# Four stages of a one-core transformer kernel: zeros sent in the first attention, scatters behind a product, slot inputs turned a span sooner, low parts a slot later

## The chip, the core and the metric

The kernel runs on one core of a Trainium2 chip. The core's engines each run their own instruction stream: TensorE (PE) multiplies matrices, VectorE (DVE), ScalarE (ACT) and GpSimd (POOL) do elementwise work, and SyncE (SP) issues most DMA transfers. They wait for each other by semaphores. The metric is the device time of one execution in microseconds. The kernel before takes 4922.42 us (median of 3 runs, 4919.28 to 4930.78).

## The reference

Four transformer layers over an activation of 4 x 1024 tokens of width 128. Each layer is `x = x + attention(norm(x)) + ffn(norm(x))`, in float32. The parts that the change touches:

- Layer 0's attention: 16 heads of width 64, softmax over 1024 keys, for 4 sequences.
- Layer 2's attention is linear: `q, k = elu(.) + 1`, `kv = k^T v`, `out = q kv / (q . sum(k) + eps)`, 16 heads of width 64.
- Layer 2's ffn is a mixture of 8 experts with top 2 and a capacity. Each token is copied to a slot of each of its two experts (at most 1024 slots per expert), the experts run over their slots, and the token gathers two weighted results:

```
disp = zeros(E * cap, D).at[flat_idx].add(x * valid)
h    = relu(disp @ fc1 + b1);  eo = h @ fc2 + b2
out  = sum(eo[flat_idx] * gates * valid)
```

- Layer 3: an attention with a recurrence over time (`S = exp(w) * S + k v`), and a mixture of 64 experts with top 8 and one shared expert, `silu(x Wg) * (x Wu)` weighted by a gate and then multiplied by `Wd`.

## The kernel before, in words

The activation is kept transposed in SBUF (`res_t`, 128 x 4096), and a normalised copy in `xn_t`. The program is a row of stages (`layer_norm`, `wide_attention`, ..., `slot_experts`, `mixing_and_experts`), each a block in which every engine has its written order of instructions, with a barrier at its end. Names in the profile have a letter for the stage: `n_` normalisation, `a_` attention, `e_` experts, `m_` the last stage. Most products are made of float16 parts: a value is split into `high` and `low`, and three matmuls (high by high, low by high, high by low) stand for one.

**Zeros.** The experts' input slots (`slots_d`, in DRAM) and their results (`y_d`) must hold zeros wherever no token lands. Between layer 0 and the second `layer_norm` a block of its own lets ACT's queue copy 4 MB of prepared rows (`slots2`) into each (L2738, L2739). `layer_norm` then loads `avg` and `ident` on SP's queue (L101, L102), and its first matmul (L114) waits for them.

**First attention** (`wide_attention`, L171). 32 units (4 sequences by 8 pairs of heads). Per unit SP issues twelve copies within SBUF (L293 to L298) that stack the parts of q and k for PE; in between SP waits.

**Linear attention** (`linear_attention`, L1057). 32 units again; `order` lists the jobs of a unit for all engines, with PE one or two units ahead in some. For unit n PE makes k, q and v (`ring`), ACT takes exponent and relu of k and q (`grown`, `clipped`), and DVE joins them (`k_s`, `q_s`, L1275), sums k over the tokens (`k_part`, L1247), and copies a product of state and output weights (`folded`, L1286). POOL multiplies q with the sum of k (`prod`, L1309); DVE reduces `prod` to the denominator and inverts it (`den`, L1254 to L1256, right behind `folded`); POOL multiplies q by it (`scaled`, two halves, L1316). PE's `state` product of the next unit waits for `folded` (L1167). Ahead of each `prod`, POOL also issues two indirect DMAs (L1302) that scatter 128 rows each of the layer's normalised tokens to their slots; they wait once for the zeros (L1299).

**Slot experts** (`slot_experts`, L2463). 8 experts, two spans of 512 slots each, and four steps per span. PE turns a span's slots (four transposes into `turned`, L2566), DVE splits it into `x_high` and `x_low` (L2666, L2668), and in each step PE makes a block of `hidden`, ACT stores it twice (`whole`, `high`), DVE makes `low` (L2679), and four steps later PE adds to `out`. The result is turned back (L2574), weighted by DVE (`y_s`, L2691) and scattered by POOL in four indirect DMAs (L2657). POOL also makes the low part of the next expert's weights (`w_low`, L2645), in the same queue. `span_at(step, j, lag)` gives the span that is due in step j of a span, `lag` spans back.

**Last stage** (`mixing_and_experts`, L1515 on). 264 steps (33 pairs of experts by 8 chunks of 512 tokens), one per slot, with the jobs of the recurrence at fixed slots between them (tables `PE_AT`, `ACT_AT`, `DVE_AT`, `POOL_AT`). Step s: PE makes gate and up products (slot s), ACT the silu (slot s, L1904), DVE the product with up (`acted`, slot s + 1, L2065), POOL the product with the gate (`scaled`, slot s + 1, L1947), ACT the high part (slot s + 2, L1898), DVE the low part (`lows`, slot s + 2, L2071), PE `out` (slot s + 4). Every third step DVE adds `out` to the activation (L1968), for which PE's next `out` waits. PE's gate product of step s waits for `acted` of step s - 2.

Of the kernel before, what the change touches and what calls it, by code (L numbers as in the profile page):

```python
# [14 lines left out]
P = 128  # L15
B, N = 4, 1024
T = B * N
# [153 lines left out]
def wide_attention(nc, stage, res_t, xn_t, w_d, w_out_d, ident_d, consts_d, scale, eps):  # L171
# [41 lines left out]
    with ExitStack() as ctx:  # L213
# [62 lines left out]
        with nc.Block() as block:  # L276
            @block.sync
            def _(eng):
# [7 lines left out]
                for n in range(units):  # L286
# [4 lines left out]
                    for h in range(2):  # L291
# [6 lines left out]
                        eng.dma_start(kb[0:64, r, h, :], nat_low["k"][own, r, :]).then_inc(stack_in[r], 16)  # L298

# [757 lines left out]
def linear_attention(nc, stage, res_t, xn_t, w_d, w_out_d, mask_d, ident_d, eps, rows, slot_of, slots_d, cleared, scattered):  # L1057
# [15 lines left out]
    with ExitStack() as ctx:  # L1073
# [51 lines left out]
        with nc.Block() as block:  # L1125
# [169 lines left out]
            def _(eng):  # L1295
# [219 lines left out]
def mixing_and_experts(nc, stage, res_t, xn_t, d, gates_d, w_d):  # L1515
# [8 lines left out]
    UP_LAG, HIGH_LAG, LAG, SPLIT_AT = 1, 2, 4, 8  # L1524
# [40 lines left out]
    with ExitStack() as ctx:  # L1565
# [105 lines left out]
        with nc.Block() as block:  # L1671
# [149 lines left out]
            def _(eng):  # L1821
# [53 lines left out]
                for slot in range(SLOTS):  # L1875
# [17 lines left out]
                    s = step_at(slot, HIGH_LAG)  # L1893
                    if s >= 0:
                        eng.wait_ge(scaled_done, s + 1)
                        if s >= HR:
                            eng.wait_ge(out_used, s - HR + 1)
                        eng.activation(high[:, s % HR, :], scaled[:, s % SR, :], ACT.Copy).then_inc(high_done, 1)  # L1898
                    s = step_at(slot, 0)
                    if s >= 0:  # L1900
# [4 lines left out]
                        if s % PER_UNIT == SPLIT_AT and s // PER_UNIT + 1 < UNITS:  # L1905
                            split(s // PER_UNIT + 1)

# [47 lines left out]
            def _(eng):  # L1955
# [101 lines left out]
                for slot in range(SLOTS):  # L2057
# [8 lines left out]
                    s = step_at(slot, HIGH_LAG)  # L2066
# [396 lines left out]
def slot_experts(nc, stage, res_t, slots_d, y_d, w_d, bias_d, ident_d, filled_sem, filled_count):  # L2463
# [7 lines left out]
    HB, HR, RING = 3, 8, 3  # L2471
# [3 lines left out]
    with ExitStack() as ctx:  # L2475
# [8 lines left out]
        x_high = pl.sb("x_high", [P, 2, BANK], F16)  # L2484
        x_low = pl.sb("x_low", [P, 2, BANK], F16)
# [27 lines left out]
        sent = [pl.sem(f"sent{r}") for r in range(2)]  # L2513
# [8 lines left out]
        with nc.Block() as block:  # L2522
# [30 lines left out]
            def _(eng):  # L2553
# [24 lines left out]
                turn_in(0)  # L2578
                for step in range(LAST):
# [16 lines left out]
                    if span_at(step, 1, -1) >= 0 and step > 0:  # L2596
                        turn_in(span_at(step, 1, -1))
# [265 lines left out]
```

## Time and profile before

| | |
|---|---|
| median of 3 runs | 4922.42 us |
| the profiled execution | 4929.4 us |
| its span | 4927.6 us |
| PE busy | 4247.0 us (86%) |
| DVE busy | 3604.9 us (73%) |
| ACT busy | 3188.9 us (65%) |
| POOL busy | 2235.6 us (45%) |

The span runs from the first to the last recorded instruction. Busy time is what an engine's instructions cover, waits left out. As the stages follow each other with barriers, the shares of the whole span say little on one stage. In the trace the second normalisation starts near 2011 us, the linear attention runs from about 3410 to 3830, the slot experts to about 4013, and the last stage from about 4050 to the end. In a row of the timeline the columns are the start and duration in us, the engine, the line and the operation, output and inputs with their shapes, how many instructions were merged, and in brackets how long the engine had been idle before, and what ended that. A queue (SPq, ACTq) issues DMAs.

### The profile page before, as it was taken

The page shows a single profiled execution, that of the slowest core. Times are in us where ns is not written, and L with a number is a line of the kernel's source. Part 1 is how long each engine was busy: PE and PEld are TensorE (multiplying, and loading weights), DVE is VectorE, ACT ScalarE, POOL GpSimd, SP SyncE. Part 2 cuts the span into 40 slices and gives each one's busy share as a digit, 9 for nine tenths or more (in the row PEclk, how much of TensorE's full clock was granted, in tenths as well). Part 3 has the DMA queues.
Part 4 walks back from the last instruction along what each step waited for, and adds up shares of the span by engine and source line. Part 5 has one row for each costly group of instructions (what it writes and reads, how often), then busy time and mean ns, then how long its engine had stood idle before and what let it go on. Part 6 is the DMA issues. An engine that isn't in the chain of part 4 may idle for free. (4 is left out here: it accounts for less than half of the span.)

```text
span 4927.6 us, 91117 instructions
## 1 busy us (share of the span) xinstructions
PE 4247.0 (86%) x35369; PEld 2321.4 (47%) x35370; DVE 3604.9 (73%) x4865; ACT 3188.9 (65%) x4796; POOL 2235.6 (45%) x1299
## 2 busy tenths in 40 slices
PE   5999999999989799677888769995877778999998
PEld 3666666666666444221211124444666343333333
DVE  5888888888845577379888947774776537888887
ACT  2777777777764599347677749992555525555554
POOL 2888888888850133200000003331555435655664
PEclk7999999999999899779999979996999879999999
DMA  2111111111100111300000011110000223334333
GB/s 62 40 40 40 40 40 41 40 39 38 37 12 1 45 65 64 104 25 14 27 18 22 14 45 44 64 43 22 12 12 13 81 81 96 90 92 100 90 96 77
DMA packets 111741, 237.30 MB, mean 48 GB/s; under 512 B 20990, under 2 KB 50942, under 8 KB 108678
## 3 DMA queue, kind: packets, MB, share of 16 engines
q1 hardware_dynamic: 98934, 214.84, 16.1%
q10 hardware_dynamic: 8304, 8.45, 0.6%
q0 software_dynamic: 4096, 8.46, 0.5%
q8 instruction: 270, 4.42, 0.4%
q14 instruction: 137, 1.11, 0.1%
HBM read 161.06 MB, written 28.75 MB: 39 GB/s over the span
## 5 line engine op out<-in xcount | busy, mean ns | idle before, releaser
L528 POOL TENSOR_TENSOR a_prob_low<-a_prob_whole,a_prob_high 128x1024 f16<-128x1024 f32 x512 | 1084.8, 2132 | 276.7 <-ACT a_prob_high L418 272.3
L502 DVE TENSOR_REDUCE a_part_max<-a_top 128x2 f32<-128x1024 f32 x512 | 626.1, 1223 | 218.5 <-PE a_top L329 212.6
L415 ACT ACTIVATE a_prob_whole<-a_score 128x1024 f32<-128x1024 f32 x512 | 525.0, 1025 | 332.5 <-PE a_score L318 320.5
L780 ACT ACTIVATE a_prob<-a_score 128x512 f32<-128x512 f32 x1024 | 532.9, 605 | 259.9 <-PE a_score L724 259.9
L813 DVE TENSOR_REDUCE a_part_max<-a_side 128x2 f32<-128x1024 f32 x512 | 595.1, 1218 | 88.1 <-PE a_side L695 88.1
L2283 DVE TENSOR_TENSOR e_low<-e_whole,e_high 128x512 f16<-128x512 f32 x544 | 453.2, 843 | 168.8 <-ACT e_high L2241 167.4
L1947 POOL TENSOR_TENSOR m_scaled<-m_acted,m_gate 128x512 f32<-128x512 f32 x264 | 402.5, 1531 | 322.3 <-DVE m_acted L2065 245.9
L418 ACT ACTIVATE a_prob_high<-a_score 128x1024 f16<-128x1024 f32 x512 | 522.3, 1020 | 0.0
L317 PE MATMUL a_score<-a_qa,a_ka 128*128 128x256 f16 x2048 | 476.2, 273 | 0.0
L318 PE MATMUL a_score<-a_qb,a_kb 128*128 128x256 f16 x2048 | 476.0, 273 | 0.0
L384 PE MATMUL a_o_ps<-a_v,a_prob_high 128*128 128x65 f16 x4096 | 428.1, 193 | 6.2 <-POOL a_prob_low L528 3.4
L2266 POOL TENSOR_TENSOR all_res_t<-all_res_t,e_gated 128x512 f32<-128x512 f32 x136 | 219.6, 1615 | 460.9 <-DVE e_gated L2292 460.6
L386 PE MATMUL a_o_ps<-a_v,a_prob_high 128*128 128x64 f16 x4096 | 426.9, 194 | 0.0
L388 PE MATMUL a_o_ps<-a_v,a_prob_low 128*128 128x65 f16 x4096 | 424.5, 192 | 0.0
L384 PEld LDWEIGHTS a_o_ps<-a_v,a_prob_high 128*128 128x128 f16 x4096 | 376.0, 96 | 85.7 <-DVE a_tokens L488 35.4
L2238 ACT ACTIVATE e_whole<-e_hidden,e_bias 128x512 f32<-128x512 f32 x544 | 383.6, 705 | 16.7 <-PE e_hidden L2190 3.0
L386 PEld LDWEIGHTS a_o_ps<-a_v,a_prob_high 128*128 128x128 f16 x4096 | 377.7, 97 | 26.9 <-issue 10.9
L2241 ACT ACTIVATE e_high<-e_hidden,e_bias 128x512 f16<-128x512 f32 x544 | 381.8, 702 | 0.0
L388 PEld LDWEIGHTS a_o_ps<-a_v,a_prob_low 128*128 128x128 f16 x4096 | 377.9, 98 | 0.0
L1898 ACT ACTIVATE m_high<-m_scaled 128x512 f16<-128x512 f32 x264 | 165.9, 628 | 288.2 <-POOL m_scaled L1947 286.1
L2071 DVE TENSOR_TENSOR m_lows<-m_scaled,m_high 128x512 f16<-128x512 f32 x264 | 239.0, 905 | 111.0 <-ACT m_high L1898 111.0
L724 PE MATMUL a_score<-a_qa,a_ka 32*128 32x512 f16 x1024 | 237.5, 398 | 90.0 <-ACT a_prob L780 87.6
(402 smaller groups left out, 10337.5 us busy)
## 6 DMA issues: line engine op xcount, KB each, us to landing
m_gate<-gates SPq DMA_DIRECT2D x264, 256.0 KB, 5.1
e_gate<-gates SPq DMA_DIRECT2D x17, 2048.0 KB, 7.1
a_ka<-a_nat_high_k SPq DMA_DIRECT2D x128, 128.0 KB, 2.4
e_w<-in_w_moe SPq DMA_DIRECT2D x25, 512.0 KB, 7.8
a_qa<-a_nat_high_q SPq DMA_DIRECT2D x64, 128.0 KB, 2.4
a_qa<-a_nat_low_q SPq DMA_DIRECT2D x64, 128.0 KB, 2.4
a_qb<-a_nat_high_q SPq DMA_DIRECT2D x64, 128.0 KB, 2.4
a_kb<-a_nat_low_k SPq DMA_DIRECT2D x64, 128.0 KB, 2.4
```

What stands on the lines that cost most here:

```text
L317: eng.matmul(score[:, e % 2, h, i, :], ka[:, r, h, keys], qa[:, r, h, qs], start=True, stop=False)
L318: mm = eng.matmul(score[:, e % 2, h, i, :], kb[:, r, h, keys], qb[:, r, h, qs], start=False, stop=True)
L384: eng.matmul(o_ps[:, at:at + V1], high, v[:, r, kt, h, 0:V1], start=(pair == 0 and i == 0 and h == 0 and t == 0), stop=False, skip_group_c ...
L386: eng.matmul(o_ps[:, at:at + DH], high, v[:, r, kt, h, V1 + 1:VW], start=False, stop=False, skip_group_check=True)
L388: mm = eng.matmul(o_ps[:, at:at + V1], low, v[:, r, kt, h, 0:V1], start=False, stop=last, skip_group_check=True)
L415: eng.activation(prob_whole[:, e % RING, :, :, :], score[:, e % 2, :, :, :], ACT.Exp, scale=scale)
L418: eng.activation(prob_high[:, e % RING, :, :, :], score[:, e % 2, :, :, :], ACT.Exp, scale=scale).then_inc(exp_done, 1)
L502: eng.tensor_reduce(part_max[:, i, c, :, qt % 4], top[:, :, :], AX.X, ALU.max).then_inc(max_done, 1)
L528: eng.tensor_tensor(prob_low[:, e % RING, :, :, :], prob_whole[:, e % RING, :, :, :], prob_high[:, e % RING, :, :, :], ALU.subtract).then_ ...
L780: eng.activation(prob[:, e % RING, h, :], score[:, step % SLOTS, :], ACT.Exp).then_inc(exp_done, 1)
L813: op = eng.tensor_reduce(part_max[:, qt // 4, c, 2 * pair:2 * pair + 2, 24 + qt], side, AX.X, ALU.max)
L2283: eng.tensor_tensor(low[:, s % HR, :], whole[:, s % HB, :], high[:, s % HR, :], ALU.subtract).then_inc(low_done, 1)
```

## The change

1. The two 4 MB copies of `slots2` no longer have a block of their own. They are cut into 16 parts of 1024 rows, and SP issues one behind the twelve stack copies of each of the units 2 to 17 of the first attention. POOL's wait in the linear attention counts 16 parts.
2. In the linear attention POOL issues `prod` ahead of the two scatters of a unit.
3. In the slot experts `turn_in` and `split_x` are done two spans ahead instead of one, `turn_in` in step 3 instead of step 1; `x_high` and `x_low` have three buffers instead of two, and `slots` four instead of three. The semaphores `sent` are now made by the caller.
4. In the last stage DVE makes `lows` of step s in slot s + 3 instead of s + 2, and ACT issues the silu of a slot ahead of the high part.

```diff
@@ wide_attention, SP
                         eng.dma_start(kb[0:64, r, h, :], nat_low["k"][own, r, :]).then_inc(stack_in[r], 16)
+                    if n >= 2:
+                        for to, source in clears[n - 2:n - 1]:
+                            eng.dma_start(to, source).then_inc(cleared, 16)
@@ linear_attention, POOL
-                eng.wait_ge(cleared, 32)
+                eng.wait_ge(cleared, cleared_count)
                 for n in range(units):
-                    for j in range(2):
-                        eng.indirect_dma_start(slots_d, bass.IndirectOffsetOnAxis(slot_of[:, j, n:n + 1], 0),
-                                               rows[:, j, n, :], None).then_inc(scattered, 16)
                     r = n % 2
                     eng.wait_ge(small_read, small["ksum", n] + 1)
...
                     eng.tensor_tensor(prod[:, :, :], q_s[:, r, :, :], k_sum[:, r, :].unsqueeze(1).broadcast_to([P, tiles, P]),
                                       ALU.mult).then_inc(multiplied, 1)
+                    for j in range(2):
+                        eng.indirect_dma_start(slots_d, bass.IndirectOffsetOnAxis(slot_of[:, j, n:n + 1], 0),
+                                               rows[:, j, n, :], None).then_inc(scattered, 16)
                     eng.wait_ge(norm, NORMS * n + 3)
@@ mixing_and_experts
-    UP_LAG, HIGH_LAG, LAG, SPLIT_AT = 1, 2, 4, 8
+    UP_LAG, HIGH_LAG, LOW_LAG, LAG, SPLIT_AT = 1, 2, 3, 4, 8
@@ mixing_and_experts, ACT: this piece moves from ahead of the silu to behind it
-                    s = step_at(slot, HIGH_LAG)
-                    if s >= 0:
-                        eng.wait_ge(scaled_done, s + 1)
...
-                        eng.activation(high[:, s % HR, :], scaled[:, s % SR, :], ACT.Copy).then_inc(high_done, 1)
@@ mixing_and_experts, DVE
-                    s = step_at(slot, HIGH_LAG)
+                    s = step_at(slot, LOW_LAG)
                     if s >= 0:
                         eng.wait_ge(high_done, s + 1)
@@ slot_experts
-    HB, HR, RING = 3, 8, 3
+    HB, HR, RING, XR = 3, 8, 4, 3
...
                 turn_in(0)
+                turn_in(1)
                 for step in range(LAST):
...
-                    if span_at(step, 1, -1) >= 0 and step > 0:
-                        turn_in(span_at(step, 1, -1))
+                    if span_at(step, 3, -2) >= 0:
+                        turn_in(span_at(step, 3, -2))
@@ slot_experts, DVE
                 def split_x(s):
-                    if s >= 2:
-                        eng.wait_ge(hidden_full, J * (s - 1))
+                    if s >= XR:
+                        eng.wait_ge(hidden_full, J * (s - XR + 1))
...
-                    if span_at(step, 2, -1) >= 0 and step > 0:
-                        split_x(span_at(step, 2, -1))
+                    if span_at(step, 2, -2) >= 0:
+                        split_x(span_at(step, 2, -2))
@@ program
+        clears = in_parts(slots_d, d["slots2"], EXPERTS * CAPACITY) + in_parts(y_d, d["slots2"][:, 0:P], 2 * T)
...
-        with nc.Block() as block:
-            @block.scalar
-            def _(eng):
-                eng.dma_start(slots_d[0:EXPERTS * CAPACITY, :], d["slots2"]).then_inc(cleared, 16)
-                eng.dma_start(y_d[0:2 * T, :], d["slots2"][:, 0:P]).then_inc(cleared, 16)
-
```

The order of the instructions, at three places. POOL at the start of the units of the linear attention, before:

```order
L1298 TENSOR_TENSOR a_w_low<-a_w,a_w_high 128x384 x8
L1302 DMA slots<-rows,slot_of 16384x130 x2
L1309 TENSOR_TENSOR a_prod<-a_q_s,a_k_sum 128x1024
L1316 TENSOR_TENSOR a_scaled<-a_q_s,a_den 128x512 x2
L1302 DMA slots<-rows,slot_of 16384x130 x2
L1309 TENSOR_TENSOR a_prod<-a_q_s,a_k_sum 128x1024
```

and now:

```order
L1301 TENSOR_TENSOR a_w_low<-a_w,a_w_high 128x384 x8
L1309 TENSOR_TENSOR a_prod<-a_q_s,a_k_sum 128x1024
L1312 DMA slots<-rows,slot_of 16384x130 x2
L1319 TENSOR_TENSOR a_scaled<-a_q_s,a_den 128x512 x2
L1309 TENSOR_TENSOR a_prod<-a_q_s,a_k_sum 128x1024
L1312 DMA slots<-rows,slot_of 16384x130 x2
```

The two scatters (`slots<-rows,slot_of`) stand between `prod` and `scaled` of a unit now, and no longer between `scaled` of the unit before and `prod`.

PE in a span of the slot experts; `e_turned` is the turning in of a coming span, `e_back` the turning back of a finished one. Before, from the middle of a step on:

```order
L2555 MATMUL e_out<-e_high,e_w_high 128x512
L2556 MATMUL e_out<-e_low,e_w_high 128x512
L2557 MATMUL e_out<-e_high,e_w_low 128x512
L2566 MATMUL e_turned<-e_ident,e_slots 128x128 x4
L2555 MATMUL e_hidden<-e_x_high,e_w_high 128x512
L2556 MATMUL e_hidden<-e_x_low,e_w_high 128x512
L2557 MATMUL e_hidden<-e_x_high,e_w_low 128x512
L2555 MATMUL e_out<-e_high,e_w_high 128x512
L2556 MATMUL e_out<-e_low,e_w_high 128x512
L2557 MATMUL e_out<-e_high,e_w_low 128x512
L2574 MATMUL e_back<-e_ident,e_o_s 128x128 x4
```

and now:

```order
L2557 MATMUL e_out<-e_high,e_w_high 128x512
L2558 MATMUL e_out<-e_low,e_w_high 128x512
L2559 MATMUL e_out<-e_high,e_w_low 128x512
L2576 MATMUL e_back<-e_ident,e_o_s 128x128 x4
L2557 MATMUL e_hidden<-e_x_high,e_w_high 128x512
L2558 MATMUL e_hidden<-e_x_low,e_w_high 128x512
L2559 MATMUL e_hidden<-e_x_high,e_w_low 128x512
L2557 MATMUL e_out<-e_high,e_w_high 128x512
L2558 MATMUL e_out<-e_low,e_w_high 128x512
L2559 MATMUL e_out<-e_high,e_w_low 128x512
L2568 MATMUL e_turned<-e_ident,e_slots 128x128 x4
```

The turning in stood one step ahead of the turning back and stands one step behind it, two steps later than before, for a span that is needed one span later.

ACT in the last stage, around a job of the recurrence (`m_low`); `m_acted` is the silu of a step. Before:

```order
L1837 ACT_TABLE_LOAD
L1837 ACTIVATE m_low<-m_work 128x512
L1898 ACTIVATE m_high<-m_scaled 128x512
L1904 ACT_TABLE_LOAD
L1904 ACTIVATE m_acted<-m_up_down 128x512
L1898 ACTIVATE m_high<-m_scaled 128x512
L1904 ACTIVATE m_acted<-m_up_down 128x512
```

and now:

```order
L1840 ACT_TABLE_LOAD
L1840 ACTIVATE m_low<-m_work 128x512
L1901 ACT_TABLE_LOAD
L1901 ACTIVATE m_acted<-m_up_down 128x512
L1909 ACTIVATE m_high<-m_scaled 128x512
L1901 ACTIVATE m_acted<-m_up_down 128x512
L1909 ACTIVATE m_high<-m_scaled 128x512
```

The silu of a slot comes ahead of the high part that stood in front of it (the first `m_high` now stands behind the second table load). DVE's rows read alike before and after there: what changes is that each `m_lows` belongs to the step before the one it belonged to.

## Rows read from the trace of the kernel before

**Rows 1.** Windows: busy us of PE, PEld, DVE, ACT, POOL; clock; DMA share; GB/s.

```profile
3440.00:3820.00 380.00, 298.81 (x3204) 248.92 (x3204) 268.07 (x316) 203.45 (x402) 222.75 (x156) 0.99 0.04 12
4130.00:4900.00 770.00, 714.35 (x2733) 300.38 (x2731) 638.35 (x830) 434.43 (x699) 460.62 (x306) 0.99 0.38 91
```

**Rows 2.** Timeline of PE, second and third normalisation.

```profile
2032.20 2.08 PE L114 MATMUL n_mean<-all_res_t,n_avg 128*128 128x512 f32 x2 [20.96 <-DMA n_ident<-in_ident]
...
3331.86 2.08 PE L114 MATMUL n_mean<-all_res_t,n_avg 128*128 128x512 f32 x2 [6.59 <-DMA n_bias<-in_bias]
```

**Rows 3.** DMA view, the second transfer of zeros: us to landing last.

```profile
y<-in_slots ACTq DMA_DIRECT2D x1, 4096.0 KB, 30.5
```

**Rows 4.** Timeline of POOL in the linear attention.

```profile
3599.58 2.37 POOL L1309 TENSOR_TENSOR a_prod<-a_q_s,a_k_sum 128x1024 f32<-128x1024 f32 x1
...
3606.42 2.81 POOL L1316 TENSOR_TENSOR a_scaled<-a_q_s,a_den 128x512 f32<-128x512 f32 x2 [4.47 <-DVE a_den L1256]
...
3611.69 2.37 POOL L1309 TENSOR_TENSOR a_prod<-a_q_s,a_k_sum 128x1024 f32<-128x1024 f32 x1
```

**Rows 5.** Timeline of ACT and DVE, same stretch and an early unit.

```profile
3609.11 0.28 ACT L1221 ACTIVATE a_k_sum<-a_small 128x128 f32<-128x128 f32 x1 [0.98 <-PE a_small L1170]
...
3610.90 0.69 DVE L1275 SCALAR_TENSOR_TENSOR a_q_s<-a_grown,a_clipped 128x512 f32<-128x512 f32 x1 [2.37 <-ACT a_clipped L1216]
...
3612.63 1.98 DVE L1275 SCALAR_TENSOR_TENSOR a_k_s<-a_grown,a_clipped 128x512 f32<-128x512 f32 x1 [1.04 <-ACT a_clipped L1216]
...
3616.53 0.28 DVE L1286 COPY a_folded<-a_small 128x128 f32<-128x128 f32 x1
...
3452.99 3.37 DVE L1275 SCALAR_TENSOR_TENSOR a_q_s<-a_grown,a_clipped 128x512 f32<-128x512 f32 x1 [2.70 <-ACT a_clipped L1216]
...
3453.96 0.60 ACT L1215 ACTIVATE a_grown<-a_ring 128x512 f32<-128x512 f32 x1 [0.51 <-PE a_ring L1158]
```

**Rows 6.** Waits of PE, 3453 to 3815: total, times, longest.

```profile
PE a_small L1167 <- DVE a_folded L1286: 41.5, 29, 2.1
```

**Rows 7.** Waits of PE in the slot experts, 3840 to 3990.

```profile
PE e_hidden L2555 <- issue: 13.4, 6, 2.2
PE e_hidden L2555 <- DVE e_x_low L2668: 12.5, 10, 2.3
```

**Rows 8.** Timeline of DVE, POOL and PE in the slot experts.

```profile
3900.84 0.68 DVE L2691 TENSOR_TENSOR e_y_s<-e_back,e_slots 128x512 f32<-128x512 f32 x1
...
3906.61 2.14 POOL L2645 TENSOR_TENSOR e_w_low<-e_w,e_w_high 128x1024 f16<-128x1024 f32 x1
...
3908.85 0.38 PE L2555 MATMUL e_hidden<-e_x_high,e_w_high 128*128 128x512 f16 x1 [2.23 <-issue]
...
3916.55 0.68 DVE L2691 TENSOR_TENSOR e_y_s<-e_back,e_slots 128x512 f32<-128x512 f32 x1
```

**Rows 9.** Source line of the scatters: ns min/median/max, first and last start.

```profile
L2657 POOL DMA_INDIRECT y<-e_y_s,e_dest x63: 952/959/1430, 3867.1 to 3988.9; - x63
```

**Rows 10.** Waits of DVE and PE in the last stage, 4130 to 4900.

```profile
DVE m_lows L2071 <- ACT m_high L1898: 106.3, 101, 3.7
PE m_out L1725 <- DVE all_res_t L1968: 20.0, 20, 3.2
PE m_up_down L1725 <- DVE m_acted L2065: 17.3, 37, 1.6
```

**Rows 11.** The page's part 5, POOL's line in the last stage.

```profile
L1947 POOL TENSOR_TENSOR m_scaled<-m_acted,m_gate 128x512 f32<-128x512 f32 x264 | 402.5, 1531 | 322.3 <-DVE m_acted L2065 245.9
```

**Rows 12.** Timeline of DVE and PE in the last stage.

```profile
4745.22 1.09 DVE L2071 TENSOR_TENSOR m_lows<-m_scaled,m_high 128x512 f16<-128x512 f32 x1 [1.23 <-ACT m_high L1898]
...
4748.96 0.39 PE L1725 MATMUL m_up_down<-m_x_high,m_w_high 128*128 128x512 f16 x1
...
4750.26 1.02 PE L1798 MATMUL m_work<-m_mixed,m_w_v 128*128 128x512 f32 x2
...
4752.55 0.39 PE L1725 MATMUL m_out<-m_high,m_w_high 128*128 128x512 f16 x1 [1.27 <-DVE all_res_t L1968]
```

More of the change, by code:

```diff
@@ L168, in layer_norm, with wide_attention @@
         pl.close()
-def wide_attention(nc, stage, res_t, xn_t, w_d, w_out_d, ident_d, consts_d, scale, eps):
+def wide_attention(nc, stage, res_t, xn_t, w_d, w_out_d, ident_d, consts_d, scale, eps, clears, cleared):
     GROUPS, DH = 8, 64
@@ L1054, in whole_attention, with linear_attention @@
         pl.close()
-def linear_attention(nc, stage, res_t, xn_t, w_d, w_out_d, mask_d, ident_d, eps, rows, slot_of, slots_d, cleared, scattered):
+def linear_attention(nc, stage, res_t, xn_t, w_d, w_out_d, mask_d, ident_d, eps, rows, slot_of, slots_d, cleared, cleared_count, scattered):
     PAIRS, DH = 8, 64
@@ L1906, in _ @@
                             split(s // PER_UNIT + 1)
+                    s = step_at(slot, HIGH_LAG)
+                    if s >= 0:
+                        eng.wait_ge(scaled_done, s + 1)
+                        if s >= HR:
+                            eng.wait_ge(out_used, s - HR + 1)
+                        eng.activation(high[:, s % HR, :], scaled[:, s % SR, :], ACT.Copy).then_inc(high_done, 1)
             @block.gpsimd
@@ L2483, in slot_experts @@
         dest = pl.sb("dest", [P, E, PER * TILES], U32)
-        x_high = pl.sb("x_high", [P, 2, BANK], F16)
-        x_low = pl.sb("x_low", [P, 2, BANK], F16)
+        x_high = pl.sb("x_high", [P, XR, BANK], F16)
+        x_low = pl.sb("x_low", [P, XR, BANK], F16)
         whole = pl.sb("whole", [P, HB, BANK])
@@ L2587, in _ @@
                             eng.wait_ge(high_done, step - HB + 1)
-                        product(hidden[:, step % HB, :], j, s // PER % 2, (x_high[:, s % 2, :], x_low[:, s % 2, :]), True, True).then_inc(hidden_full, 1)
+                        product(hidden[:, step % HB, :], j, s // PER % 2, (x_high[:, s % XR, :], x_low[:, s % XR, :]), True, True).then_inc(hidden_full, 1)
                     k = step - LAG
@@ L2716, in program @@
         scattered = pl.sem("scattered")
+        sent2 = [pl.sem(f"sent2{r}") for r in range(2)]
         slots_d = nc.dram_tensor("slots", (EXPERTS * CAPACITY + 2 * T, P + 2), F32, kind="Internal").ap()
@@ L2724, in _, with in_parts @@
                 eng.wait_ge(x_in, 16)
+        def in_parts(to, source, rows):
+            part = 2 * BANK
+            return [(to[at:min(at + part, rows), :], source[at:min(at + part, rows), :]) for at in range(0, rows, part)]
+        clears = in_parts(slots_d, d["slots2"], EXPERTS * CAPACITY) + in_parts(y_d, d["slots2"][:, 0:P], 2 * T)
         layer_norm(nc, "n0", res_t, xn_t, d["avg"], d["ident"], d["bias0"])
-        wide_attention(nc, "a0", res_t, xn_t, d["w_qkv0"], d["w_o0"], d["ident"], d["rowmask0"], scale=64 ** -0.5, eps=1e-10)
+        wide_attention(nc, "a0", res_t, xn_t, d["w_qkv0"], d["w_o0"], d["ident"], d["rowmask0"], scale=64 ** -0.5, eps=1e-10,
+                       clears=clears, cleared=cleared)
         with nc.sbuf_tensor("xp_t", [P, T], F32) as xp_t:
```

14 lines of the change are left out of this document (6 added, 8 removed).

## The prediction

> **What bounds the kernel now.** I read the busy time by stretch first [rows 1]. The kernel is a row of stages with a barrier between them, so each edit is priced in its own stage. DMA bounds neither of the two long stretches: its share is 0.04 and 0.38. In the linear attention (3440 to 3820) no engine is full: PE is busy for 299 of 380 us. In the last stage (4130 to 4900) PE is busy for 714.35 of 770, so 55.65 us are idle, and it is the nearest to a PE bound. Then I read, in each, who ends PE's waits and what that one was doing, which is where the terms below come from.
>
> **1. The zeros leave the gap before the second normalisation.** The first matmul of n1 comes after 20.96 us of idle PE, ended by the load of a 64 KB constant; in n2, which follows the same kind of stage, the gap is 6.59 [rows 2]. The difference is two transfers of 4 MB each, issued ahead of that load; the second lands 30.5 us after its issue [rows 3]. Without them n1's gap should be n2's: 20.96 - 6.59 = 14.4 us less. It is a plain serial gap, nothing else runs in it. Bounds: 13 (the constants are issued a little later than in n2) to 15.
>
> They now go out as 16 parts of about 0.5 MB on SP's queue in the first attention, one behind the twelve copies of a unit. Both transfers together took 30.5 us, so a part takes about 1.9 us (30.5 / 16), and the next unit's copies are a whole unit away. SP stands idle there and nobody waits for a part until the scatters. I take 0. If each part held a transfer that PE waits for through its whole 1.9 us, the price would be 30 us; a gain has no source.
>
> **2. Scatters behind the product in the linear attention.** POOL's round is scaled, two scatters, prod, and the scatters fill its time between scaled and prod [rows 4]. The period is 3611.69 - 3599.58 = 12.11 us. The scatters take the time from 3609.23 (end of scaled) to 3611.69. The input of prod is there earlier: ACT's k_sum ends at 3609.39 [rows 5]. So prod will start about 3609.45, 2.2 us sooner, and end at 3611.8 instead of 3614.06. What does that give? The den reduction that reads prod starts only after DVE's folded at 3616.53, so nobody waits for prod itself. But DVE's k_s at 3612.63 takes 1.98 us, against 0.69 for the same operation on q_s [rows 5]: it reads two operands in SBUF while prod does, and ends 0.55 us after prod ends. k_part and folded follow it back to back, and PE waits for folded in 29 units, 41.5 us in all, or 1.43 each [rows 6]. With prod over at 3611.8, k_s finds POOL away from its operands and takes 0.69: 1.98 - 0.69 = 1.29 us less per unit.
> What is late next: q_s, ready at 3610.90, now falls under prod and ends about 3612.35 instead of 3611.6, still ahead of k_s at 3612.63. An early unit shows this case: q_s took 3.37 us under prod, and ACT's next grown began at 3453.96 in the middle of it, so ACT does not wait there [rows 5]. PE's wait of 1.43 just covers the 1.29, so PE comes to the same point with 0.1 to spare. 31 periods by 1.29 = 40 us. Bounds: 0 (PE's own chain holds the period, or DVE's work moves under another POOL operation), 43 (all of PE's wait, 1.43 by 30).
> The scatters then stand beside k_s and k_part and end about 3614.1; scaled cannot start before 3617.2: folded would begin at 3616.53 - 1.29 = 3615.24, and scaled begins 2.0 us after it (3606.42 against 3616.53 - 12.11). So they have 3 us of room.
> The Trainium skill, SBUF — State Buffer, section "SBUF: two separate sides", speaks against this: a DMA issued from GpSimd has its descriptors written by GpSimd, which some DVE operations lock out, and it quotes about 3.1 us for a scatter that takes 0.62 alone. By that figure, an estimate, two scatters would take 6 us and end past den. The row says less: 63 scatters in the slot experts, where DVE does its low parts from two operands in SBUF beside them, take 0.96 us in the median and 1.43 at most [rows 9]. By these the two take 3 us at the worst, which is the room.
>
> **3. Inputs turned a span sooner in the slot experts.** PE's hidden product waits for x_low 10 times, 12.5 us, and 6 times for 13.4 us more that the view calls issue [rows 7]. The second kind is POOL's: w_low ends at 3906.61 + 2.14 = 3908.75 and hidden starts at 3908.85 [rows 8]. That is a loop through two spans: y_s ends at 3901.52, four scatters and w_low take until hidden at 3908.85 (7.3 us), and the next y_s ends at 3917.23 (8.4 us on), 15.7 per expert. The x wait at the middle of an expert is not on this loop, so taking it away only makes the wait for w_low longer. What is gained is at the ends: the first two waits come before the loop closes (one is the longest, 2.3; the other I put at 1.5, the rest having 10.2 / 9 = 1.1 in the mean), and an estimated 2 us go at the end, where the last two x waits no longer hold back scatters that run back to back. What is lost: DVE's split now waits for a transpose that PE issues two steps later (after step 3 instead of 1), right in front of low and y_s, which are on the loop. That costs between 0 and 1.4 us per expert (two operations of 0.68 in a row); my chain of DVE and PE operations gives 0.5. Six loops: +3. Sum: -3.8 - 2 + 3 = -3. Bounds: -12.5 (all x waits go) to +6.
>
> **4. Last stage.** DVE waits 101 times for ACT's high, 106.3 us; and high waits for POOL's scaled [rows 10]. In DVE's order the low part of step s comes behind the product of step s+1, so when DVE is late it does two products in a row and then stands still until POOL (1.53 in the mean [rows 11]) and ACT have gone round: at 4745.22 1.23 us of idle and then a low part of 1.09, and shortly behind it PE's out product waits 1.27 us for DVE's addition [rows 12]. A slot later the high part is long there, and DVE issues the low part right behind the product, before POOL gets the operands. ACT does the silu before it waits for POOL. PE's waits on DVE of 0.2 us and more are of this kind: 20.0 us on the addition, 17.3 on the product [rows 10]. The whole of PE's idle is 55.65; part comes from bursts of DVE work alone (scan, reciprocal). I take 33, about 0.6 of it, since both kinds of wait make 37 and not every one goes. Bounds: 0 to 50. The cover that the edit uses up: out of step s-4 has one DVE slot less of lead; its low part follows 0.7 us behind the event that frees PE's hidden, whose two products take 1.30 (from 4748.96 to 4750.26) [rows 12], so it is hidden with 0.6 to spare.
>
> **Sum.** -14.4 + 0 - 40 - 3 - 33 = -90.4. The profiled execution took 4929.4 (span 4927.6), giving 4839.0. The median of the runs is 7.0 below the profiled one, so 4832.
>
> **Rivals.** (A) DVE's waits in the last stage only turn into waits for its own bursts and PE gains 8 instead of 33: 4857. For it: the stalls cluster around scan and reciprocal. Against: those bursts start late because of the waits for high. (B) The linear attention's period is held by PE or ACT and gives half: 4852. For: only 0.1 us to spare. Against: the early unit. (C) The parts of zeros hold loads or code that PE needs in the first attention, +30: 4862. For: in n1 a load on the other queue was held for the whole transfer. Against: then 8 MB were queued at once. (D) Scatters held until DVE's run ends at den: they take 2.3 us from there, and scaled, which is on the loop, moves by that: instead of -1.29 the period grows by 1.0. 4832 + 40 + 31 = 4903. (E) Slower: out waits for the low part in each step. If the low part stands behind POOL's scaled (1.53) as it can now after a wait, it ends about 2.2 us behind the product, and PE's 1.3 us of hidden no longer cover it: from 0.7 us of delay on it decides, and at 0.6 us for each of 264 steps costs 158: 4832 + 33 + 158 = 5023. Against: wherever the low part is ready, it starts ahead of POOL.
>
> **Numbers.** The forecast holds with 0.60, A 0.14, B 0.12, C 0.06, D 0.03, E 0.04, and 0.01 for an edit without effect. The forecast's own range is 4805 to 4855. The low end of all is the gains at their bounds, 15 + 43 + 12 + 50 = 120: 4802. With A, B and C inside, the range is 4803 to 4872; D, E and mixtures are outside. 0.2% is 10 us, about what a measurement of this kernel can tell from no change: faster holds for all but E and the last, 0.94; same 0.02; slower 0.04.
>
> **What would show it.** n1's gap near 6.5 us; the first attention as long as before. In the linear attention a period of 10.8 us, k_s at 0.69, q_s near 1.4, PE's wait for folded near 0.1. In the slot experts no waits for x_low but longer ones for w_low, at about 16 us per expert. In the last stage DVE's wait for high near nothing, PE idle near 25 us, no wait for the low part. A period that stays above 11.5, or PE's waits of 40 us and more in the last stage, would make the forecast wrong.

## Result and profile after

The changed kernel takes 4842.05 us (median of 4 runs, 4833.08 to 4845.46) against 4924.36 before (4 runs, 4919.28 to 4930.78): ratio 0.9829, 95% interval 0.9811 to 0.9847, which is 84 us less (75 to 93). The forecast was 4832, with 4803 to 4872 as its range. The profiled execution took 4833.1, span 4831.2; the forecast for it was 4839.0.

| stretch | before | after | moved | forecast |
|---|---|---|---|---|
| start to first matmul of n1 | 2032.2 | 2016.4 | -15.8 | -14.4 |
| n1 to n2 (second attention, first experts) | 1299.7 | 1293.5 | -6.2 | 0 |
| n2 to last `a_out` of the linear attention | 496.3 | 450.4 | -45.9 | -40 |
| from there to n3 (slot experts) | 190.5 | 194.4 | +3.9 | -3 |
| n3 to the end | 908.9 | 876.5 | -32.4 | -33 |

PE's timeline at the starts of the second and third normalisation answers to [rows 2]; the rows of the DMA view on the zeros (KB each, us to landing) answer to [rows 3]:

```profile
2016.36 4.33 PE L114 MATMUL n_mean<-all_res_t,n_avg 128*128 128x512 f32 x6 [5.69 <-DMA n_ident<-in_ident]
...
3309.82 4.42 PE L114 MATMUL n_mean<-all_res_t,n_avg 128*128 128x512 f32 x6 [6.92 <-DMA n_bias<-in_bias]
```

```profile
slots<-in_slots SPq DMA_DIRECT2D x8, 520.0 KB, 4.0
...
y<-in_slots SPq DMA_DIRECT2D x8, 512.0 KB, 4.2
```

The gap is 5.69 us instead of 20.96. A part of the zeros lands about 4 us after its issue.

The windows of the linear attention and of the last stage, columns as in [rows 1]:

```profile
3419.00:3750.00 331.00, 292.14 (x3190) 247.98 (x3187) 251.01 (x316) 198.61 (x400) 228.00 (x156) 0.99 0.04 14
...
4065.00:4806.00 741.00, 706.30 (x2738) 303.07 (x2737) 654.93 (x830) 426.37 (x699) 491.16 (x307) 1.00 0.39 95
```

PE is idle for 38.9 of 331 us and for 34.7 of 741 us, where it was 81.2 of 380 and 55.65 of 770 before. A unit of the linear attention on POOL, DVE and ACT, for [rows 4, 5]:

```profile
3568.50 2.36 POOL L1309 TENSOR_TENSOR a_prod<-a_q_s,a_k_sum 128x1024 f32<-128x1024 f32 x1 [0.23 <-ACT a_k_sum L1224]
3571.01 1.27 POOL L1312 DMA_INDIRECT slots<-rows,slot_of  x1 [0.15 <-issue]
3572.59 0.96 POOL L1312 DMA_INDIRECT slots<-rows,slot_of  x1 [0.30 <-issue]
3576.03 2.80 POOL L1319 TENSOR_TENSOR a_scaled<-a_q_s,a_den 128x512 f32<-128x512 f32 x2 [2.48 <-DVE a_den L1259]
3579.07 2.36 POOL L1309 TENSOR_TENSOR a_prod<-a_q_s,a_k_sum 128x1024 f32<-128x1024 f32 x1 [0.23 <-ACT a_k_sum L1224]
```

```profile
3569.93 1.47 DVE L1278 SCALAR_TENSOR_TENSOR a_q_s<-a_grown,a_clipped 128x512 f32<-128x512 f32 x1 [2.37 <-ACT a_clipped L1219]
3571.40 0.69 DVE L1278 SCALAR_TENSOR_TENSOR a_k_s<-a_grown,a_clipped 128x512 f32<-128x512 f32 x1
3572.20 1.93 DVE L1250 TENSOR_REDUCE a_k_part<-a_k_s 128x128 f32<-128x1024 f32 x1
3574.04 0.28 DVE L1289 COPY a_folded<-a_small 128x128 f32<-128x128 f32 x1
...
3575.86 0.63 DVE L1278 SCALAR_TENSOR_TENSOR a_q_s<-a_grown,a_clipped 128x512 f32<-128x512 f32 x1
```

```profile
3568.14 0.28 ACT L1224 ACTIVATE a_k_sum<-a_small 128x128 f32<-128x128 f32 x1 [0.98 <-PE a_small L1173]
...
3570.74 0.63 ACT L1219 ACTIVATE a_clipped<-a_ring 128x512 f32<-128x512 f32 x1
```

The period is 3579.07 - 3568.50 = 10.57 us instead of 12.11. PE's wait for `folded` [rows 6] is gone from the list of its waits; of the waits long enough for the view to list only one is left in the middle units (total, times, longest):

```profile
PE a_small L1173 <- DVE a_state_t L1284: 34.6, 29, 2.1
```

In the slot experts the waits for x_low [rows 7] are gone and all is what the view calls issue. The waits of PE there, and one of them in the timelines of POOL, DVE and PE:

```profile
PE e_hidden L2557 <- issue: 26.4, 7, 4.3
```

```profile
3854.80 2.13 POOL L2648 TENSOR_TENSOR e_w_low<-e_w,e_w_high 128x1024 f16<-128x1024 f32 x1
...
3854.14 3.35 DVE L2683 TENSOR_TENSOR e_low<-e_whole,e_high 128x512 f16<-128x512 f32 x1
...
3857.03 0.59 PE L2557 MATMUL e_hidden<-e_x_high,e_w_high 128*128 128x512 f16 x1 [4.33 <-issue]
3857.41 0.63 PE L2558 MATMUL e_hidden<-e_x_low,e_w_high 128*128 128x512 f16 x1
```

PE starts 0.10 us after w_low ends (3856.93), as in [rows 8]. The waits of the last stage, DVE's and PE's, for [rows 10]:

```profile
DVE m_acted L2068 <- ACT m_acted L1901: 39.2, 34, 4.6
DVE all_res_t L1971 <- PE m_out L1730: 32.5, 26, 2.3
DVE m_lows L2074 <- ACT m_high L1909: 4.1, 5, 0.9
```

```profile
PE m_out L1728 <- DVE all_res_t L1971: 11.7, 12, 3.3
PE m_work L1804 <- DVE m_rs L2028: 9.2, 7, 1.5
PE m_up_down L1728 <- DVE m_acted L2068: 7.1, 16, 0.7
```

DVE's wait for high fell from 106.3 to 4.1 us, PE's two waits on DVE from 37.3 to 18.8.

### The profile page after: what moved, and what is told of

It is laid out like the page before. It is cut to its first block and busy times, and to the rows that moved or that the text cites. A ratio compares the mean times of both kernels' runs of the same rounds, so it can differ in the third digit from the quotient of the medians.

```text
span 4831.2 us, 91118 instructions
## 1 busy us (share of the span) xinstructions
PE 4225.0 (87%) x35369; PEld 2321.0 (48%) x35370; DVE 3616.8 (75%) x4865; ACT 3173.7 (66%) x4796; POOL 2273.3 (47%) x1299
## 5 line engine op out<-in xcount | busy, mean ns | idle before, releaser
L1950 POOL TENSOR_TENSOR m_scaled<-m_acted,m_gate 128x512 f32<-128x512 f32 x264 | 433.4, 1650 | 270.0 <-DVE m_acted L2068 201.6
L1901 ACT ACTIVATE m_acted<-m_up_down 128x512 f32<-128x512 f32 x264 | 157.4, 596 | 319.5 <-PE m_up_down L1730 318.9
L739 PE MATMUL a_o_ps<-a_prob,a_v 128*32 128x512 f32 x2048 | 285.9, 632 | 14.0 <-ACT a_raw L772 14.0
```

Of the source, the lines that this page charges most:

```text
L1950: eng.tensor_tensor(scaled[:, s % SR, :], acted[:, s % AR, :], gate[:, g % 2, j, c % 2 * BANK:(c % 2 + 1) * BANK], ALU.mult).then_inc(scal ...
```

## Experiments

Each was timed in five rounds beside the kernel before; ratios are to it.

**One edit at a time.** Four kernels, each the kernel before with one part of the change.

```diff
@@ zeros_only
+                    if n >= 2:
+                        for to, source in clears[n - 2:n - 1]:
+                            eng.dma_start(to, source).then_inc(cleared, 16)
@@ scatter_only: this piece moves from ahead of prod to behind it
                     for j in range(2):
                         eng.indirect_dma_start(slots_d, bass.IndirectOffsetOnAxis(slot_of[:, j, n:n + 1], 0),
@@ slots_only
-    HB, HR, RING = 3, 8, 3
+    HB, HR, RING, XR = 3, 8, 4, 3
-                    if span_at(step, 1, -1) >= 0 and step > 0:
-                        turn_in(span_at(step, 1, -1))
+                    if span_at(step, 3, -2) >= 0:
+                        turn_in(span_at(step, 3, -2))
@@ last_only, and ACT's silu ahead of its high part
+    UP_LAG, HIGH_LAG, LOW_LAG, LAG, SPLIT_AT = 1, 2, 3, 4, 8
```

> Only the first edit, on the kernel before. Own-gap theory: the gap before the second normalisation goes from 21.0 to about 5.7 us, and the normalisation itself is 2.4 us shorter since PE comes to it without a long idle, so 17 to 18 us less, about 4907; the first attention as long as before. Rival, the parts hold copies in the first attention: that stage is up to 30 us longer and the kernel about 4935. Rival, the 4 us that the second attention and its experts were shorter in the changed kernel come from the zeros too: 22 us less, 4902.

> Only the second edit. Theory (k_s no longer under the product): period of the linear attention 10.6 us instead of 12.1, k_s at 0.69, 46 us less, about 4878. Rival, a part of what the changed kernel shows there comes from the zeros being long landed or from the other edits: 20 to 30 us less, a period above 11.

> Only the third edit. Theory (a loop over y_s, four scatters and w_low holds the stage; the x waits were off it, and the later split puts work in front of y_s): 4 us more, about 4928, with no waits for x_low and about 26 us of waits for w_low. Rival, the edit gains what PE waited for x_low, 12 us, and something else in the changed kernel took it back: 4912.

> Only the fourth edit. Theory (DVE no longer waits for high): 32 us less, about 4892, DVE's waits for high from 106 to about 4 us. Rival, the last stage gains only together with an earlier start or a higher clock from the stages ahead: 10 to 20 us less.

| | median | ratio (95%) | in us |
|---|---|---|---|
| zeros_only | 4916.43 | 0.9973 (0.9963 to 0.9983) | -13 |
| scatter_only | 4879.30 | 0.9902 (0.9887 to 0.9917) | -48 |
| slots_only | 4930.77 | 1.0008 (0.9999 to 1.0017) | +4 |
| last_only | 4894.71 | 0.9931 (0.9918 to 0.9945) | -34 |

They sum to -92 against -84 (-75 to -93) for all together, so within the intervals the stages add up, and nothing shows that one edit needs another. The zeros alone give 13 (8 to 18), where I expected 17 to 18: the gap is 5.88 us, but the normalisation behind it starts as slowly as before, in PE's timeline:

```profile
2017.38 5.49 PE L114 MATMUL n_mean<-all_res_t,n_avg 128*128 128x512 f32 x6 [5.88 <-DMA n_ident<-in_ident]
```

In zeros_burst (below), with the same gap, the same six took 4.29 us. Over all profiled executions the six took 5.12 to 5.49 us in the seven kernels with the long gap; of the seven with the short one three took 5.49 and four 4.29 to 4.56. So the short gap does not by itself make that normalisation 2.4 us shorter, as I had expected; whether it makes it likelier these few executions don't show. Nor is the -6.2 of the table an effect: from the first product of the second attention to the last hidden product of the first experts, where all these kernels run the same code, the profiled executions of these four take 1245.4 us (last_only) to 1252.1 (zeros_only), the kernel before 1249.8 and the changed one 1245.7.

**The zeros all at once.** As zeros_only, with all 16 parts behind the copies of unit 2:

```diff
-                    if n >= 2:
-                        for to, source in clears[n - 2:n - 1]:
+                    if n == 2:
+                        for to, source in clears:
```

> As zeros_only, but all 16 parts of the zeros go out in a row behind the twelve copies of unit 2 of the first attention. Theory (the queue is idle for the rest of the unit, 42 us against 30 for the zeros): the first attention is as long as before, the kernel takes what zeros_only took, about 4915. Rival (the copies of unit 3 or the fetching of instructions stand behind the burst): the first attention is 5 to 30 us longer, 4920 to 4945.

Measured 4916.55, ratio 0.9979 (0.9970 to 0.9988), as zeros_only within the intervals. SP issues the parts from 146.7 to about 171 us; the last `a_score` of `a_qa` in the first attention starts at 1421.1 us, at 1421.6 in the kernel before and at 1420.7 in the changed one. The cover is whole even for 8 MB in a row; spreading them was not needed. In the source view (ns min/median/max of an issue, first and last start):

```profile
L301 SPq DMA_DIRECT2D slots<-in_slots x8: 488/589/1760, 146.7 to 151.5; - x8
L301 SPq DMA_DIRECT2D y<-in_slots x8: 591/1832/7013, 153.3 to 170.5; - x8
```

**One scatter ahead of the product, one behind.**

```diff
-                    for j in range(2):
-                        eng.indirect_dma_start(slots_d, bass.IndirectOffsetOnAxis(slot_of[:, j, n:n + 1], 0),
-                                               rows[:, j, n, :], None).then_inc(scattered, 16)
+                    eng.indirect_dma_start(slots_d, bass.IndirectOffsetOnAxis(slot_of[:, 0, n:n + 1], 0),
+                                           rows[:, 0, n, :], None).then_inc(scattered, 16)
...
                                       ALU.mult).then_inc(multiplied, 1)
+                    eng.indirect_dma_start(slots_d, bass.IndirectOffsetOnAxis(slot_of[:, 1, n:n + 1], 0),
+                                           rows[:, 1, n, :], None).then_inc(scattered, 16)
```

> On the kernel before: of the two scatters of a unit the first stays ahead of prod, the second goes behind it. Theory (what counts is whether prod is over when k_s starts): prod starts about 1.3 us sooner and ends at the start of k_s, so nearly the whole gain of the second edit is there already, 35 to 42 us, about 4888. Rival (what counts is POOL's own time between scaled and prod, or the scatters' time there): half of the 48 us, about 4903.

Measured 4905.18, ratio 0.9959 (0.9945 to 0.9973): 20 us less (13 to 27), where the theory had 35 to 42. My theory as I had put it fell. A unit in the timelines of POOL and DVE:

```profile
3615.71 2.37 POOL L1308 TENSOR_TENSOR a_prod<-a_q_s,a_k_sum 128x1024 f32<-128x1024 f32 x1
...
3616.19 2.46 DVE L1275 SCALAR_TENSOR_TENSOR a_q_s<-a_grown,a_clipped 128x512 f32<-128x512 f32 x1 [2.37 <-ACT a_clipped L1216]
3618.57 0.68 DVE L1275 SCALAR_TENSOR_TENSOR a_k_s<-a_grown,a_clipped 128x512 f32<-128x512 f32 x1
3619.35 1.91 DVE L1247 TENSOR_REDUCE a_k_part<-a_k_s 128x128 f32<-128x1024 f32 x1
```

The same unit on ACT, and the row of the kernel before that belongs to it (for [rows 5]):

```profile
3614.40 0.28 ACT L1221 ACTIVATE a_k_sum<-a_small 128x128 f32<-128x128 f32 x1 [0.98 <-PE a_small L1170]
...
3617.00 0.63 ACT L1216 ACTIVATE a_clipped<-a_ring 128x512 f32<-128x512 f32 x1
```

```profile
3612.00 0.59 ACT L1216 ACTIVATE a_clipped<-a_ring 128x512 f32<-128x512 f32 x1
```

k_s is at 0.68, as the theory wanted, and yet half of the gain is missing: q_s now starts inside prod and is held to 0.57 us after prod's end (3618.08), and k_s comes behind it. In all three kernels the DVE operation that lies under prod ends 0.54 to 0.57 us after prod: k_s before (3614.61 against 3614.06 [rows 4, 5]), q_s here and q_s in the changed kernel (3571.40 against 3570.86).

What moves the period is the end of k_s. Counted from the start of ACT's k_sum, k_s ends after 5.50 us before, 4.85 here and 3.95 in the changed kernel, that is 0.65 and 1.55 sooner, and the period is 12.11, 11.45 (3615.71 - 3604.26) and 10.57: 0.66 and 1.54 less. Two things must be over before k_s can start, q_s on DVE and ACT's clipped, and the rows say which one was last:

| from the start of k_sum, us | clipped ends | q_s ends | k_s starts |
|---|---|---|---|
| before | 3.48 | 2.48 | 3.52 |
| one_ahead | 3.23 | 4.25 | 4.17 |
| changed kernel | 3.23 | 3.26 | 3.26 |

Before it was clipped, here it is q_s. In the changed kernel both end at nearly the same point, and k_s starts 0.03 us behind clipped, as it did before (right behind a q_s it is recorded 0.08 us ahead of that one's end, as here). By this reading, which no run tests, moving prod still further away would gain nothing more there: ACT would hold k_s at the same place. That clipped comes 0.25 us sooner than before in both kernels is measured; why it does is not. This reading was made after the result. The rival that counts POOL's time (half each) gives a total of 24 us, which the interval allows, but not these rows, in which it is q_s that is late.

**The two halves of the last edit.** Both on the kernel before. In swap_only ACT's high part of a slot moves behind the silu, as in the change, and `LOW_LAG` is 2; low_only is DVE's half:

```diff
-    UP_LAG, HIGH_LAG, LAG, SPLIT_AT = 1, 2, 4, 8
+    UP_LAG, HIGH_LAG, LOW_LAG, LAG, SPLIT_AT = 1, 2, 3, 4, 8
...
-                    s = step_at(slot, HIGH_LAG)
+                    s = step_at(slot, LOW_LAG)
                     if s >= 0:
                         eng.wait_ge(high_done, s + 1)
```

> On the kernel before: ACT's order of the fourth edit alone (silu ahead of the high part), DVE's low part stays in slot s + 2. Theory (the gain is DVE's: it no longer stands at the low part): the high part comes later and DVE waits for it as long or longer, 0 to 20 us slower, 4928 to 4948. Rival (the gain is ACT's: silus are no longer held behind the wait for POOL): 10 to 20 us faster.

> On the kernel before: DVE's low part in slot s + 3 alone, ACT's order stays. Theory: DVE's waits for high go from 106 us to under 15 and most of the gain is there, 20 to 33 us, about 4900. Rival (both halves are needed, since ACT's silus stay behind the wait for POOL and DVE's product then waits for them): under 15 us.

low_only: 4899.59, ratio 0.9944 (0.9931 to 0.9958), 28 us less, as the theory said. swap_only: 5009.59, ratio 1.0164 (1.0150 to 1.0178), 81 us slower; the direction was right, the size four times my upper end. DVE's, ACT's and PE's waits in swap_only:

```profile
DVE m_lows L2071 <- ACT m_high L1906: 205.0, 155, 5.0
```

```profile
ACT m_acted L1898 <- PE m_up_down L1727: 387.4, 205, 6.4
```

```profile
PE m_out L1725 <- DVE all_res_t L1968: 48.6, 38, 3.5
PE m_up_down L1725 <- DVE m_acted L2065: 45.7, 57, 1.9
```

ACT stands at the silu until PE has made the gate and up products; the high part is behind it, DVE's low part waits for that, and the product that PE waits for is behind the low part. In low_only DVE waits for the silu instead, 53.9 us; in last_only, which has the swap as well, it is still 50.0, and 39.2 in the changed kernel. Whether the swap is worth anything once the low part is a slot later isn't shown: last_only gained 34 us (27 to 40) and low_only 28 (21 to 34).

```profile
DVE m_acted L2065 <- ACT m_acted L1904: 53.9, 50, 4.6
```

**The weights' low part off the path of the slot experts.** On the changed kernel, for ACT's w_high and POOL's w_low:

```diff
-        w_high = pl.sb("w_high", [P, 2, 2 * J, P], F16)
-        w_low = pl.sb("w_low", [P, 2, 2 * J, P], F16)
+        w_high = pl.sb("w_high", [P, 3, 2 * J, P], F16)
+        w_low = pl.sb("w_low", [P, 3, 2 * J, P], F16)
...
-                        if step % (J * PER) == J and s // PER + 1 < E:
+                        if step % (J * PER) == 0 and s // PER + 1 < E:
...
-                    if step % (J * PER) == J and e + 1 < E:
+                    if step % (J * PER) == 0 and e + 1 < E:
```

> On the changed kernel: in the slot experts w_high and w_low have three buffers instead of two, and both are made four steps sooner (step 0 of an expert instead of step 4), so that w_low doesn't stand behind scatters right ahead of the next expert. Theory (the loop over y_s, scatters and w_low holds the stage): the 26 us of waits for w_low go and the stage is 20 to 26 us shorter, about 4820. Rival (DVE or ACT hold it at nearly the same pace): under 8 us.

Measured 4808.79, ratio 0.9763 (0.9750 to 0.9777), by the ratios about 33 us less than the changed kernel: the best of all, and more than expected. From the first to the last hidden product, changed kernel and then w_early, columns as in [rows 1]:

```profile
3774.00:3907.20 133.20, 106.83 (x480) 52.07 (x478) 86.46 (x112) 89.83 (x147) 65.78 (x57) 0.87 0.23 73
```

```profile
3779.50:3874.20 94.70, 93.72 (x481) 49.19 (x479) 78.51 (x111) 87.22 (x145) 64.47 (x55) 0.98 0.34 103
```

PE is nearly full. Of the 38.5 us gained, 25.4 were idle time of PE and 13.1 are its own work, at a granted clock of 0.98 instead of 0.87 (106.83 us by 0.87/0.98 would be 94.8, near the 93.72 measured). About 5 us come back before the last stage's products. A second measurement, beside the next ones:

> w_early once more, beside w_early_turn1 on the same chip: 4809 again, within 5 us.

4810.58, ratio 0.9761 (0.9747 to 0.9774).

**Does the third edit pay there?** w_early_turn1 is w_early with the third edit undone; w_early_ring4 has the fourth buffer of slots given back:

```diff
@@ w_early_turn1
-    HB, HR, RING, XR = 3, 8, 4, 3
+    HB, HR, RING = 3, 8, 3
-                    if span_at(step, 3, -2) >= 0:
-                        turn_in(span_at(step, 3, -2))
+                    if span_at(step, 1, -1) >= 0 and step > 0:
+                        turn_in(span_at(step, 1, -1))
@@ w_early_ring4, on w_early_turn1
-    HB, HR, RING = 3, 8, 3
+    HB, HR, RING = 3, 8, 4
```

> As w_early, but with the inputs turned as in the kernel before (one span ahead, in step 1; two buffers of x, three of slots). Theory (with w_low off the path the waits for x_low decide, which cost 12.5 us in the kernel before): 10 to 15 us slower than w_early, about 4820, with the waits for x_low back. Rival (the third edit is worth nothing either way, as it was alone): within 4 us of w_early, about 4809.

> w_early_turn1 with four buffers of slots instead of three; the inputs still turned one span ahead, in step 1, with two buffers of x. Theory (the 46 us by which w_early_turn1 is slower than w_early are SP's: with three buffers the load of slots waits for y_s and holds the load of the next weights behind it, so that ACT waits 4.7 us per expert): 30 us or more of them go, about 4820. Rival (the place of the turning and the two buffers of x cost them): under 10 us go, about 4850.

w_early_turn1: 4856.08, ratio 0.9860 (0.9844 to 0.9875), 46 us slower than w_early and slower than the changed kernel. Neither expectation held. x_low is late, but in the timeline of SP's queue the load of weights stands right behind the load of slots, which waits for y_s (y_s ends at 3830.23), and ACT waits for those weights:

```profile
3830.26 0.36 SPq L2530 DMA_DIRECT2D e_slots<-slots  x1
3830.66 0.58 SPq L2535 DMA_DIRECT2D e_w<-in_w_moe  x1
```

```profile
3835.76 1.06 ACT L2620 ACTIVATE e_w_high<-e_w 128x1024 f16<-128x1024 f32 x1 [4.62 <-DMA e_w<-in_w_moe]
```

With the fourth buffer (w_early_ring4) 4826.88, ratio 0.9794 (0.9780 to 0.9807): 29 of the 46 us were the buffer's. The other 16 are the place of the turning and the third buffer of x together, which no run takes apart. So the third edit, worth nothing alone, is worth 46 us once w_low is off the path. PE's waits in w_early_ring4:

```profile
PE e_hidden L2557 <- DVE e_x_low L2670: 18.9, 15, 2.3
```

## Why the prediction was right, and where it was not

**Zeros: right.** -15.3 us in the gap against -14.4, nothing in the first attention against 0 (its last `a_score` at 1420.7 us against 1421.6), shown by zeros_only and, for the cover, by zeros_burst. Rival C fell.

**Scatters: right in mechanism, the term too small.** Forecast -1.29 per unit, measured -1.54 (46.5 over 31 periods by the first and last prod, 3440.84 to 3817.67 before and 3419.2 to 3749.5 now, and 48 in the timing of the edit alone), just outside my bound of 43. The step that failed is "1.98 - 0.69 = 1.29 us less": a difference of two durations, which leaves the start of k_s where it was, at 3612.63. The start moved too. k_s had waited for ACT's clipped, and that ends 3.23 us after the start of k_sum now, where it ended after 3.48 [rows 5, and the row shown with one_ahead]; these 0.25 us and the 1.29 make the 1.54. The forecast had q_s end at 3612.35, 3.24 after k_sum, and it does (3.26). So nothing in the forecast's account of prod was wrong; what it had not asked is whether the other thing that k_s waits for would also move. The rest came as forecast: q_s 1.47 (forecast near 1.4), k_s 0.69, PE's wait for `folded` too short for the view to list. Rival B (half) fell. Rival D would have made the scatters late, and so would the rule of the Trainium skill that I weighed (SBUF — State Buffer, "SBUF: two separate sides", descriptors locked out), whose figure of 3.1 us is for a DMA beside DVE's `tensor_copy`. The scatters took 1.27 and 0.96 us with q_s, k_s and k_part beside them and ended 2.5 us ahead of `scaled`. The same page's section "Who interferes with whom" says that a DVE instruction with two SBUF inputs contends with a GpSimd instruction that reads SBUF and that the second to issue blocks until the first is done. For q_s and k_s under prod the traces agree, to about 0.55 us behind prod's end; by the recorded starts it does not hold for `low` in the slot experts (last section).

**Slot experts: wrong in sign, within the bounds.** -3 forecast, +3.9 in the traces and +4 (0 to +8) for slots_only. The loop was right: PE's waits are all behind w_low, with nothing gained inside. The step that failed is the price of the loop, "my chain of DVE and PE operations gives 0.5" per expert. From one w_low to the next an expert takes (3892.32 - 3799.16) / 5 = 18.6 us, against (3957.10 - 3871.95) / 5 = 17.0 before: +1.6. I had read the loop (15.7) from one expert, the shortest of the five, when the others took 17.3 and 17.4, and the windows say what sets that one apart. Two rounds before and two now, from the hidden product that follows a w_low to the next such one, columns as in [rows 1]:

```profile
3908.85:3924.56 15.71, 12.45 (x65) 6.43 (x66) 10.10 (x16) 12.00 (x19) 10.37 (x9) 1.00 0.32 101
3924.56:3941.96 17.40, 14.13 (x65) 6.87 (x66) 10.11 (x16) 12.00 (x19) 9.87 (x9) 0.90 0.30 92
```

```profile
3838.84:3857.03 18.19, 13.86 (x64) 6.89 (x65) 11.96 (x16) 11.78 (x19) 10.58 (x9) 0.88 0.29 87
3857.03:3876.36 19.33, 14.99 (x64) 7.22 (x65) 11.97 (x16) 11.78 (x19) 10.14 (x9) 0.85 0.27 83
```

The short round is the one in which PE kept its full clock. In the other PE does the same work in 14.13 us instead of 12.45, and these 1.68 us are the whole difference between the two. In the eight traces with this stage as it was before, 11 of 40 rounds have a granted clock of 1.00 and take 15.7 us; the other 29 take 17.3 to 17.4. In the changed kernel each of the five rounds has a stretch at half clock, in the last one shown 5.57 us long (last section). Such a stretch costs half of its length, 2.8 us, so by an estimate the loop at full clock is 19.33 - 2.8 = 16.5 us, 0.8 above 15.7, where I had 0.5. By this about half of the +1.6 per expert is that chain and the rest the clock, which the sum left out: PE now stands still for 4.33 us in one piece behind each w_low, where it had stood for 2.23 there and again for x_low. No run holds the clock fixed, so the split is worked out and not tested.

From the first y_s to the last it makes +7.9 (116.3 to 124.2). The start gave 5.8 instead of 3.8 (first hidden product to first y_s, 24.9 to 19.1), a second turning ahead of the first product cost 0.7, and the end cost 1.1 instead of giving 2. w_early shows the size of what stood there: 33 us of the kernel.

**Last stage: right, the closeness in part luck.** -32.4 against -33; -34 for the edit alone. Rival A, 8 instead of 33, fell. The balance inside differs. From the first gate product to the last, PE was idle for 61.7 of 805.9 us (4098.1 to 4904.0) and is for 39.8 of 774.7 (4034.8 to 4809.5): 21.9 us of the 31.2 are idle time, and 9.3 are PE's own recorded work, which the forecast had taken as unchanged. The granted clock rose from 0.99 to 1.00 (0.993 to 0.998 in the trace), which by an estimate makes 3 of the 9.3; the rest stays open. In the window shown 34.7 us are idle, where I had said near 25. low_only shows that DVE's order carries it. Rival E, slower by a part that each step waits for, is what half of this edit does: swap_only, with ACT's high in place of the low part, is 81 us slower. I had the swap down as a small gain of its own; alone it is a large loss, since it makes high late for a low part that still waits in the next slot.

**Sum.** The deltas were -90.4 forecast and -96.4 in the profiled executions, of which 6.2 lie between n1 and n2 and differ from one execution to the next. That the rest comes so near is partly luck: the linear attention gained 6 us more than forecast and the slot experts came out 7 worse. For the medians it is, by the ratio, -84 (-75 to -93) where the forecast's median implies -90.4. The base that I took, 4922.42, is at the low side of what later runs gave (4924 to 4929), and the profiled execution of the changed kernel was its fastest. Both lie inside the scatter of single executions, about 12 us.

## What to carry to other kernels

Where one engine holds another's operation, work out when the held one will end, from everything that it waits for: the holder's end, what queues ahead of it, its input. Ask of each whether it moves too; the difference of the held one's durations leaves its start where it was. Where a wait is ended now by one engine and now by another, look for the loop through all of them and measure its period over several rounds, with the granted clock of each; only what lies on the loop pays, and here it was the weights' low part behind four scatters. And an edit of two engines' orders is priced by its halves: one half can be a large loss that the other prevents.

## What the runs showed of the hardware

- DVE operations of 128x512 with two SBUF operands that were held by a POOL operation ended 0.54 to 0.57 us after it, however long they had taken by then: q_s at 2.46 and 1.47, k_s at 1.98, `low` at 3.35.
- Who was recorded as started first does not say who is held. `low` that had started 0.66 us ahead of w_low (3854.14 against 3854.80, alone 0.69 long) was held to 0.56 us after its end, and so in all six rounds of the changed kernel. In slots_only, where `low` was over as w_low began (3867.59 + 0.68 against 3868.27), it took 0.68. But the q_s that starts 0.17 us ahead of `scaled` (3575.86 against 3576.03) took its 0.63, in 31 units, and was not held. What decides stays open. The holding of `low` did not lengthen the stage: from the first hidden product to the last slots_only took 134.0 us, the changed kernel 133.2.
- After PE's wait of 4.33 us the granted clock was 0.50 (1.2 GHz) for the next 5.6 us, then 1.00 (2.4 GHz) again. Behind the shorter waits of 2.23 to 2.24 us of the kernel before it went both ways: in one of five rounds the clock stayed at 1.00 [rows 8], the other four had a mean of 0.90 or 0.91. The windows of the first case, columns as in [rows 1]:

```profile
3857.03:3862.60 5.57, 5.57 (x14) 1.99 (x15) 1.99 (x4) 2.53 (x4) 3.32 (x4) 0.50 0.72 221
3863.00:3868.00 5.00, 5.00 (x29) 2.82 (x28) 2.64 (x6) 4.34 (x8) 0.14 (x1) 1.00 0.05 16
```
